# Seven-product blocks: the sixth product in front of the fifth, the conditioning of the second half between the fifth and the seventh

## The reference

```
w = weights[conditions]                       # 128 samples, a 64x64 matrix each
c = einsum('bct,bcd->bdt', x, w)              # "conditioning"; x is (128, 64, 512)
h = gelu(einsum('bsd,hd->bsh', c, ternarize(W1)) + b1)      # 512 -> 2048
y = einsum('bsd,hd->bsh', h, ternarize(W2)) + b2            # 2048 -> 512
out = x + fp4_activation(y)                   # scale = max|y| / 7 + 1e-8, over all of y
```

## Time and profile before

| | us |
|---|---|
| median of 3 runs | 992.52 (992.35 to 992.72) |
| the profiled execution | 992.28 |
| its span, from the first to the last instruction | 990.5 |
| TensorE busy | 907.8 (92%) |
| VectorE busy | 690.1 (70%) |
| ScalarE busy | 617.1 (62%) |
| GpSimd busy | 158.8 (16%) |

### The profile page before, as it was taken

How to read it: one execution, slowest core, us unless ns; L and a number is a source line. 1 busy time by engine, 2 the same in 40 slices (tenths; PEclk the granted TensorE clock), 3 DMA queues, 4 the chain that set the end, 5 groups by cost and what they waited for, 6 DMA issues and landing times.

```text
span 990.5 us, 15837 instructions
## 1 busy us (share of the span) xinstructions
PE 907.8 (92%) x5822; PEld 506.6 (51%) x5822; DVE 690.1 (70%) x1141; ACT 617.1 (62%) x718; POOL 158.8 (16%) x180
## 2 busy tenths in 40 slices
PE   2999999999999999999999999999999999999700
PEld 2544444766657584857667444444444444444300
DVE  7997859899797979898997464555455454423493
ACT  6887836768494948677684837466473745336190
POOL 4400221121304030121203203030301200000000
PEclk9999999999999999999999999999999999999955
DMA  9501221221204040212203022120303110204899
GB/s 339 161 2 43 48 50 47 50 48 39 57 0 95 0 93 3 53 42 48 48 16 81 7 51 46 42 53 17 77 1 68 27 42 0 85 0 182 308 385 396
DMA packets 24333, 78.06 MB, mean 79 GB/s; under 512 B 3952, under 2 KB 4080, under 8 KB 23792
## 3 DMA queue, kind: packets, MB, share of 16 engines
q1 hardware_dynamic: 20032, 73.41, 24.8%
q0 software_dynamic: 3840, 3.94, 1.7%
q10 hardware_dynamic: 432, 0.34, 0.1%
HBM read 60.89 MB, written 16.78 MB: 78 GB/s over the span
## 4 chain that ended last, share of the span: by engine, by line
PE 73%; issue 16%; DVE 6%; ACT 2%; DMA 1%; POOL 0%; DVEq 0%; SPq 0%; POOLq 0%; ACTq 0%
PE ps L493 36%; PE ps L609 18%; PE ps L503 14%; PE ps L554 3%; PE ps L472 2%; ACT y L869 1%; DVE st L1014 1%; DVE st L1083 1%; DVE wts L1341 1%; DMA yx<-in_x 1%; DVE wts L935 1%; DMA odd<-in_itok_B 1%; DVE y L1222 1%; DVE y L1341 0%; ACT g L726 0%
## 5 line engine op out<-in xcount | busy, mean ns | idle before, releaser
L493 PE MATMUL ps<-yc,wts 128*128 128x512 f16 x2048 | 444.8, 379 | 0.0
L493 PEld LDWEIGHTS ps<-yc,wts 128*128 128x128 f16 x2048 | 200.3, 98 | 240.1 <-DVE y L940 0.3
L503 PE MATMUL ps<-wts 128*128 128x512 f16 x896 | 197.4, 381 | 0.0
L935 DVE SCALAR_TENSOR_TENSOR wts<-g,st,wts 128x512 f16<-128x512 f32 x144 | 106.6, 750 | 117.5 <-ACT wts L731 112.4
L726 ACT ACTIVATE g<-ps,b1t,st 128x512 f32<-128x512 f32 x144 | 112.0, 778 | 108.7 <-PE ps L493 97.5
L503 PEld LDWEIGHTS ps<-wts 128*128 128x128 f16 x896 | 87.1, 98 | 103.7 <-issue 2.3
L386 POOL DMA_INDIRECT odd<-in_L_cond_weights,odd x112 | 130.8, 1168 | 46.6 <-issue 31.8
L830 ACT ACTIVATE g<-ps,b1t,st 128x512 f32<-128x512 f32 x112 | 86.0, 771 | 41.6 <-PE ps L493 33.1
L731 ACT ACTIVATE wts<-g,st 128x512 f16<-128x512 f32 x144 | 101.6, 712 | 0.0
L403 POOL PARTITION_ALL_REDUCE st<-st x32 | 13.7, 429 | 530.6 <-DVE st L957 393.6
L609 PE MATMUL ps<-y,wts 128*128 128x256 fp8e4 x672 | 75.6, 272 | 0.0
(11 more groups left out here) (165 smaller groups left out, 858.6 us busy)
## 6 DMA issues: line engine op xcount, KB each, us to landing
yx<-in_x SPq DMA_DIRECT2D x42, 512.0 KB
y<-in_x SPq DMA_DIRECT2D x14, 512.0 KB
wts<-in_x SPq DMA_DIRECT2D x10, 512.0 KB, 5.5
out<-wts SPq DMA_DIRECT2D x10, 512.0 KB, 13.8
y<-in_L_ffn_W SPq DMA_DIRECT2D x8, 512.0 KB, 8.0
wts<-in_x SPq DMA_DIRECT2D x4, 1024.0 KB, 5.3
y<-in_L_ffn_W SPq DMA_DIRECT2D x4, 1024.0 KB, 20.4
y<-in_x SPq DMA_DIRECT2D x3, 1024.0 KB, 9.3
```

The source lines that it names most:

```text
L493: last = nc.tensor.matmul(psH[:, j % HB, :], T1T[:, h // HC, k, h % HC * P:(h % HC + 1) * P], csp[:, a, k, :], start=(k == 0 and a == 0), ...
L503: last = nc.tensor.matmul(psY[:, r % 2, :], hsp[:, a, j, r * P:(r + 1) * P], T2T[:, j, :], start=(j == 0 and a == 0), stop=(j == HT - 1 an ...
L935: nc.vector.scalar_tensor_tensor(out=hsp[:, 1, j, :], in0=g[:, j % HB, :], scalar=s_h, in1=hsp[:, 0, j, :], op0=ALU.mult, op1=ALU.subtract ...
```

## The change

TensorE made products 0 to 3, the conditioning of the second half, and products 4, 5, 6. It now makes products 0 to 3, product 5, product 4, the conditioning of the second half, and product 6. Product 5 gets a wait for read 1 (which frees bank 1) and a fence of its own; product 6 waits for one read more than before, since two reads stand between product 4's result and the count. VectorE reads in the new order: product 5 (the fifth made) from bank 1, product 4 (the sixth made) from bank 0, and then bank 1 a second time for the other quarter. All three reads now stand in front of `low_c`, `max_w` and `scale_xw` of the second half; before, one stood between `low_c` and `max_w`, and two behind `scale_xw`.

```diff
@@ tensor, seven_step
                 fence()
                 seven(s, 3, told, 2, wsum[:, 1], 0, False)
-                condition(i + 1, 1)
+
+                pe.wait_ge(m_read, 8 * s + 3)
+                fence()
+                seven(s, 5, told, 0, wsum[:, 0], 1)
                 pe.wait_ge(m_read, 8 * s + 5)
                 fence()
                 seven(s, 4, told, 1, wsum[:, 2], 0, False)
-                seven(s, 5, told, 0, wsum[:, 0], 1)
-                pe.wait_ge(m_read, 8 * s + 6)
+                condition(i + 1, 1)
+                pe.wait_ge(m_read, 8 * s + 7)
                 seven(s, 6, told, 3, A22, 0, False)
@@ vector, seven_step
                 read(3, 3, 0, 0, 0, behind=2)
                 low_x(2 * i, 0)
+                read(4, 4, 1, 0, 0, behind=3)
+                read(5, 5, 0, 0, 1)
+                read(6, 4, 1, 0, 1, behind=5)
                 low_c(i + 1, 1)
-                read(4, 4, 0, 0, 1)
                 max_w(2 * i + 1, 1, i + 2)
                 scale_xw(2 * i + 1, 1, lk)
-                read(5, 5, 1, 0, 0, behind=3)
-                read(6, 5, 1, 0, 1, behind=4)
```

## The result

| | before | changed |
|---|---|---|
| median, us | 992.43 (4 runs, 992.25 to 992.72) | 998.86 (4 runs, 997.98 to 999.33) |
| ratio | | 1.0063 (1.0048 to 1.0078) |
| the profiled execution | 992.28 | 999.33 |
| its span | 990.5 | 997.5 |

The change costs 6.4 us, 0.6%. The forecast was 1002.8, in a range of 996.5 to 1006.5. The profiled execution took 7.05 more than the one before (999.33 against 992.28), the median of the runs 6.4 more.

What follows compares the result with a forecast made beforehand. TensorE bounded the kernel; after the change a loop through ScalarE, GpSimd and VectorE would, 56.7 us against 54.89. Six periods add 10.9, the ends -0.4: 992.28 + 10.9 - 0.4 = 1002.8 us, range 996.5 to 1006.5.

Steps and rivals of the forecast that it cites:

- a new wait in product 0: TensorE waits about 2 us for VectorE's last low part, six times, a few matmuls before product 0's end.
- copy to the hidden stage's start: From ScalarE's copy of the second half's conditioning, through sum, all-reduce, high and low parts and read 7: 12.56 us.
- to the last low part's end: VectorE's hidden stage, 25.59 us before, less 0.80 of idle time given back: 24.79 us.
- to the conditioning of the next block: TensorE's last four matmuls of product 0, then products 1, 2, 3, 5 and 4 with hop and fences.
- conditioning to copy: From product 4's end, where the conditioning now follows, to ScalarE's next copy: 1.4 us, bounds 1.2 and 1.6.
- what the hidden stage gives back: Idle time VectorE can recover within its hidden stage: 0.80 us, bounds 0 and 1.2.
- VectorE is busy 17.30 of 17.30: Mid hidden stage VectorE has no idle time, so a delay at the stage's start stays to its end.
- paragraph on a rule: Weighed the skill's pipe-emptying rule against the trace; claimed VectorE can't go faster than 3.45 us a pair.
- partly absorbed: Rival: hidden stage gives back 1.5 to 2 us or the copy comes sooner; 995.5, up to 999; chance 0.09.
- the case given 0.75: The forecast itself: the longer loop sets the period, 999 to 1006 us; chance 0.75.
- Product 6's stall: TensorE waits for read 5 ahead of product 6: 0.75 us, bounds 0 and 1.07, costing nothing by itself.
- product 0's slack: Before the change, VectorE's last low part ends 0.9 us before product 0's last four matmuls need it.

Runs made afterwards that it cites:

- Experiment 4: Kernel before, with two unused maxima (1.2 to 1.3 us) added on VectorE in each seven-product block: 987.15 us, 0.9998 of the 987.4.
- experiment 7: Changed kernel with the absolute sum of the second half of x made earlier, max_w and scale_xw moved forward: 1006.86 us, ratio 1.0136.
- experiment 5: Kernel before, with GpSimd's gather of the second half's matrices issued in front of the first half's all-reduce: 986.75 us, ratio 0.9944.
- experiment 6: Changed kernel, with GpSimd's gather of the second half's matrices issued in front of the first half's all-reduce: 998.65 us, 1.0060 of the kernel before.
- experiment 9: Kernel of experiment 8, with the gather of the next first half held back until product 6 is done: 987.75 us, ratio 0.9951.
- experiment 8: Kernel of experiment 7, with the second half's gather also issued in front of the first half's all-reduce: 1003.60 us, ratio 1.0112.
- experiment 2: Kernel before, old product order, second half's conditioning moved between products 5 and 6, three reads in front of low_c: 1006.44 us, ratio 1.0194.
- experiment 1: Changed kernel with the second half's conditioning back between products 5 and 4, low_c and max_w before read 5: 993.53 us, 1.0063 of the 987.4.
- experiment 3: Changed kernel, with two unused maxima (1.2 to 1.3 us) added on VectorE in each seven-product block: 1005.34 us, 1.0182 of the 987.4.

## Why the prediction was right

The mechanism, the place and the sign were right: a loop that is longer than TensorE's own work, and by it a new wait in product 0, six times. The terms of the loop against the trace:

| from, to | forecast | measured |
|---|---|---|
| copy to the hidden stage's start | 12.56 | 271.02 - 258.44 = 12.58 |
| to the last low part's end | 24.79 | 295.36 - 271.02 = 24.34 |
| to the conditioning of the next block | 17.97 | 313.57 - 295.36 = 18.21 |
| conditioning to copy | 1.4 | 258.44 - 257.47 = 0.97 |
| period | 56.7 | 56.1 |

*Two terms were too large, by 0.45 and 0.43.* The first is what the hidden stage gives back. From the stage's start to its second low part it was 3.84 before (266.79 to 270.63) and is 2.94 now (271.02 to 273.96): 0.90 given back, where the forecast had 0.80. The other six pairs took 20.73 before and take 20.39 now (273.96 to 294.35), 3.40 each in place of 3.45. That is another 0.34, which the forecast put at nothing. The reason was that "VectorE is busy 17.30 of 17.30", and this was a misreading: before, each L1203 started 0.65 behind its L1198 (276.89 and 277.54), now 0.60 (276.75 and 277.36), and the profile lists no idle time for the difference. So 3.45 was TensorE's pace (27.63 / 8), and VectorE had 0.05 a pair in hand. The prediction's paragraph on a rule drew from it that VectorE can't go faster than 3.45; the 3.40 shows that it can. Together the stage gives back 25.59 - 24.34 = 1.25, just over the upper bound of 1.2.

The second is the 1.4 from the conditioning to the copy. It held 0.4 of the same lateness as read 3: the row was taken from a block in which the conditioning itself took longer than its 0.93.

*One term was too small, by 0.24:* from the last low part to the next conditioning, TensorE took 18.21 and not 17.97, most of it in the first 68 matmuls (7.60 for 7.43). In all the loop is 0.6 shorter than forecast, six times 3.7 us, and that is the miss (3.9 in the median, 3.5 in the profiled execution).

*A part of it is the width of the range.* The loop came out 56.10 - 54.89 = 1.2 longer than the period before, and not 1.8. The prediction's rival "partly absorbed" ends at this very number (999 at 1.2), and the case given 0.75 begins at 999. So the time stands on the border of the two: the path was the forecast one, and about a third of the forecast excess was absorbed, by the hidden stage and by the sooner copy, as that rival says.

*Product 6's stall* was forecast at 0.75 and is 0. Read 5 started 0.16 behind its product, and not 0.5 to 1.2 as read 3 had. I had taken the nearest row for the price of "a read under a conditioning"; it was the price of read 3's lateness. This is a second step in which the reason was wrong. It cost little (0.75 once, behind the last loop), and the lower bound in the text had it.

*The lateness of VectorE, from end to end.* The stage starts 9.09 behind product 6's end (261.93), where it was 4.88: 4.2 later, not 3.9, since product 6 didn't stall. Of this the stage gives back 1.25, product 0's slack takes about 1, and 1.87 is what TensorE stands. Experiment 4 shows the same from the other side: the 1.12 us by which its stage begins later are given back within the stage and don't even touch the slack.

*The rule on the most-contended engine* (the Trainium skill, Perfetto Trace Analysis, "Identifying the Most-Contended Engine") says to optimize the engine with the highest occupancy first, though it adds that TensorE's matmul busy time is no good measure of the headroom left. By occupancy it would have picked TensorE's 92%. In the changed kernel TensorE is still the busiest, 908.8 of 997.5 us, but its share of the chain that ended last fell from 73% to 51% of the span.

## What to carry to other kernels

Before work is moved later behind a bottleneck engine, follow what hangs on its result around the loop, through every queue, to the point where the same engine needs it again. Compare the sum with the period. What is in hand on the way (here 1.25 us in the hidden stage and about 1 in front of product 0's last matmuls) decides whether the move costs anything, and the share of busy time doesn't show it. A second engine that is busy for 100% of a stage may only be keeping the first one's pace: here it caught up 0.34 us in six pairs, which is little against the 4.2 that it was late, and the busy rows didn't show even that.

A wait is length and lateness. Where a wait is worth covering, first ask why the releasing and the released row are further apart than elsewhere: one moved gather gave 5.7 us (986.75), and the new order with its loop shortened and both gathers moved gave no more than that (987.75).

## What was not expected

An instruction can start late while GpSimd's indirect transfers run beside it, though what it waits for has long been done: read 3 by 0.5 to 1.2 us in the kernel before, ScalarE's copy by 3.4 in experiment 7. Moving the gather away took it away both times (experiments 5, 6 and 9). It isn't one engine that is late: in the kernel before TensorE pauses within the conditioning, with no releaser, in two of the seven blocks (0.29 us up to 250.26, where read 3 starts at 250.42), and in experiment 8 its pause ends with ScalarE's. Why stays open. It isn't the gather alone: in experiment 2, on another chip, read 3 was prompt with the gather in its old place, as in the kernel of experiment 4. Nor is it x's transfer alone: in experiment 9 this ran beside the prompt copy. The profile gives no releaser that explains the delay. The Trainium skill (Runtime: NRT & Kernel Launch, "Instruction fetch mechanics") says that a branch to code outside the engine's small instruction memory makes it wait for a fetch by DMA. No run here shows that this happened: the list of DMA queues has no instruction packets in the window of the late copy, and a kernel that moves the code's place without moving a gather wasn't tried.

The kernel before takes 992.5 us on some chips and 987.4 on another, 0.5% apart, which is more than its runs differ on one chip. A prompt read 3 is worth about as much (5.7 us in experiment 5), and read 3 was prompt in the traces of experiments 1 to 4, all from the third chip. So the ratio of a change that covers read 3 should depend on the chip. That was not measured: the changed kernel wasn't timed there.
